# Attention stage of a fused four-layer kernel: a separate order of steps for TensorE, VectorE and ScalarE

## The reference

```python
def _L0_attn_ref(x, Wq, Wk, Wv):
    q = jnp.einsum('bsh,oh->bso', x, Wq)
    k = jnp.einsum('bsh,oh->bso', x, Wk)
    v = jnp.einsum('bsh,oh->bso', x, Wv)
    scores = jnp.einsum('bqh,bkh->bqk', q, k) / jnp.sqrt(jnp.float32(H))
    scores = jnp.where(causal[None, :, :], scores, -jnp.inf)
    att = jax.nn.softmax(scores, axis=-1)
    return jnp.einsum('bqk,bkh->bqh', att, v)

x = x + _L0_attn_ref(_layernorm(x, axis=-1), L0_attn_Wq, L0_attn_Wk, L0_attn_Wv)
```

## Time and profile before

| | before |
|---|---|
| median of 3 executions | 2508.66 us (2501.77 to 2509.47) |
| the profiled execution's own time | 2511.11 us |
| its span | 2509.4 us |
| TensorE matmuls, busy | 2360.6 us (94%) |
| VectorE, busy | 1791.1 us (71%) |
| ScalarE, busy | 1291.6 us (51%) |
| GpSimd, busy | 701.0 us (28%) |
| mean granted TensorE clock | 0.97 |

### The profile page before, as it was taken

One profiled execution on the slowest core, in us unless ns is written; L12 is line 12 of the kernel. 1 busy time (PEld: TensorE's weight loads), 2 busy tenths in 40 slices (PEclk: granted clock), 3 DMA queues, 4 the chain that ended last, 5 costly groups with the idle time before them and its releaser, 6 DMA issues.

```text
span 2509.4 us, 43786 instructions
## 1 busy us (share of the span) xinstructions
PE 2360.6 (94%) x16024; PEld 2182.2 (87%) x16024; DVE 1791.1 (71%) x3323; ACT 1291.6 (51%) x2027; POOL 701.0 (28%) x468
## 2 busy tenths in 40 slices
PE   7999995899999969999999999998999999999999
PEld 6888885899999968988988988987988998899998
DVE  5776775899999866565575574665788787877774
ACT  4445443344444325464464554564666665655554
POOL 1111111444454423023123122122344442321110
PEclk9999997999999989999999999996999999999999
DMA  5000000000000000000000000002000010000001
GB/s 182 0 0 0 0 0 20 1 0 0 0 0 0 1 17 1 13 8 13 13 4 17 13 4 17 8 13 81 26 18 22 20 50 28 1 26 26 25 25 34
DMA packets 43259, 45.69 MB, mean 18 GB/s; under 512 B 3120, under 2 KB 41904, under 8 KB 43184
## 3 DMA queue, kind: packets, MB, share of 16 engines
q1 hardware_dynamic: 43184, 44.69, 5.5%
HBM read 27.90 MB, written 16.78 MB: 18 GB/s over the span
## 4 chain that ended last, share of the span: by engine, by line
PE 51%; DVE 5%; issue 3%; ACT 2%; POOL 1%; DVEq 0%; ACTq 0%; POOLq 0%
PE m_ps_z L1859 12%; PE p_ps_a L1641 4%; PE p_ps_feat L279 4%; PE p_ps_a L1698 4%; PE p_ps_feat L281 3%; PE p_ps_feat L280 3%; PE m_ps_wide L279 3%; PE m_ps_wide L281 3%; PE m_ps_wide L280 3%; PE p_ps_a L1579 2%; PE p_ps_turn L1685 2%; PE m_ps_wide L1837 1%; PE m_ps_wide L1838 1%; PE m_ps_n L1820 1%; PE p_ps_b L279 1%
## 5 line engine op out<-in xcount | busy, mean ns | idle before, releaser
L1951 DVE TENSOR_TENSOR m_a_lo<-m_a,m_a_hi 128x512 fp32r<-128x512 f32 x256 | 201.2, 803 | 144.0 <-ACT m_a_hi L1911 140.1
L1859 PE MATMUL m_ps_z<-m_w_hi,m_a_hi 128*128 128x256 f32 x1024 | 290.7, 284 | 1.5 <-DVE m_a_lo L1951 0.9
L1859 PE MATMUL m_ps_z<-m_w_hi,m_a_lo 128*128 128x256 f32 x1024 | 288.0, 281 | 0.0
L1859 PEld LDWEIGHTS m_ps_z<-m_w_hi,m_a_hi 128*128 128x128 f32 x1024 | 192.3, 188 | 13.5 <-DVE d_w_lo L2468 1.9
L1859 PEld LDWEIGHTS m_ps_z<-m_w_hi,m_a_lo 128*128 128x128 f32 x1024 | 192.7, 188 | 0.0
L1907 ACT ACTIVATE m_a<-m_ps_wide,d_b,d_w_gain 128x512 f32<-128x512 f32 x128 | 99.8, 780 | 135.8 <-PE m_ps_wide L281 131.7
L1324 POOL TENSOR_TENSOR p_kf<-p_kf,p_k_shift 128x1024 f32<-128x1024 f32 x64 | 119.4, 1903 | 155.5 <-DVE p_k_shift L1459 155.5
L1859 PE MATMUL m_ps_z<-d_w_lo,m_a_hi 128*128 128x256 f32 x512 | 144.7, 283 | 0.0
L1859 PE MATMUL m_ps_z<-m_w_lo,m_a_hi 128*128 128x256 f32 x512 | 143.6, 280 | 0.0
L1641 PE MATMUL p_ps_a<-p_ctx_pair,p_kf 128*128 128x34 f32 x1024 | 128.4, 283 | 0.0
L1641 PEld LDWEIGHTS p_ps_a<-p_ctx_pair,p_kf 128*128 128x128 f32 x1024 | 127.7, 203 | 0.4
(11 more groups left out here) (350 smaller groups left out, 8027.4 us busy)
## 6 DMA issues: line engine op xcount, KB each, us to landing
residual<-in_x SPq DMA_DIRECT2D x8, 1024.0 KB, 11.8
attn<-p_attn SPq DMA_DIRECT2D x32, 256.0 KB, 2.2
m_attn<-attn SPq DMA_DIRECT2D x16, 512.0 KB, 3.8
out<-residual SPq DMA_DIRECT2D x16, 512.0 KB, 2.9
raw_weights<-in_d_q SPq DMA_DIRECT2D x2, 1024.0 KB, 7.2
m_attn<-in_d_scale SPq DMA_DIRECT2D x3, 512.0 KB, 4.0
raw_weights<-in_m_w1T SPq DMA_DIRECT2D x1, 1024.0 KB, 5.0
raw_weights<-in_m_w2T SPq DMA_DIRECT2D x1, 1024.0 KB, 7.9
```

Of the source, the lines that this page charges most:

```text
L1859: mm = pe.matmul(z, a, w[:, f, :], start=(f == 0 and k == 0 and j % 2 == 0), stop=(f == FC - 1 and k == 2), skip_group_check=True)
L1951: dve.tensor_tensor(self.a2[1][:, f, :], self.a[f % RING][:, :], self.a2[0][:, f, :].bitcast(F32), ALU.subtract).then_inc(self.a_lo, 1)
```

## The change

VectorE gets an order of its own, and the steps that `schedule` used to append are now in the tables, so that each engine can place them freely. TensorE's order stays the same step by step.

```diff
-        ORDER = "s2 s3 t0 t1 n0 s4 w0 w1 n1 t2 t3 s5 w2 w3 n2 t4 s6 w4 t5 n3 n4 s7 t6 w5 n5 n6"
-
-        ORDER_OF_SCALAR = "s2 s3 t0 t1 t2 s4 t3 s5 t4 s6 t5 n3 n4 s7 t6 n5 n6"
+        ORDER_OF_TENSOR = "s2 s3 t0 t1 s4 w0 w1 t2 t3 s5 w2 w3 t4 s6 w4 t5 s7 t6 w5 T0 T1 w6 t7 P0 P1 w7 T2 T3"
+        ORDER_OF_VECTOR = "s2 s3 t0 t1 N0 s4 t2 w0 t3 w1 s5 N1 w2 w3 N2 t4 s6 w4 t5 s7 t6 w5 T0 T1 w6 t7 P0 P1 w7 T2 T3"
+        ORDER_OF_SCALAR = "s2 s3 t0 t1 t2 s4 t3 s5 t4 s6 t5 N3 N4 t6 s7 T0 T1 N5 N6 t7 P0 P1 T2 T3"
         STEPS = {"s": "scores", "t": "turn", "w": "weigh"}
...
-        def schedule(tile, front, skip_turn, order=ORDER):
+        def schedule(tile, front, skip_turn, order):
...
-                    else:
-                        ahead(e)
-                ahead("t0", "t1")
-                tile(b, "weigh", TB - 2)
-                tile(b, "turn", TB - 1)
-                ahead("p0", "p1")
-                tile(b, "weigh", TB - 1)
-                ahead("t2", "t3")
+                    elif not last:
+                        front(b + 1, e[0].lower(), int(e[1:]))
```

More of the change, by code:

```diff
@@ L434, in body @@
             def body(b, last):
[L435 to L438, removed]
                 def beside(m):
@@ L619, in _ @@
             dve.sem_inc(fp4_weights.quantised, 1)
-            schedule(tile, front, lambda eng: skip_uses(eng, turned_lo))(dve)
+            schedule(tile, front, lambda eng: skip_uses(eng, turned_lo), ORDER_OF_VECTOR)(dve)
         @block.scalar
@@ L746, in front @@
                     mm.then_inc(proj_done, 1)
-            schedule(tile, front, lambda eng: skip_uses(eng, turned))(pe)
+            schedule(tile, front, lambda eng: skip_uses(eng, turned), ORDER_OF_TENSOR)(pe)
         core.ctx = outer
```

## The result

| | before | after |
|---|---|---|
| median | 2508.10 us (2501.77 to 2509.47, 6 executions) | 2491.18 us (2486.83 to 2495.17, 6 executions) |
| span of the profiled execution | 2509.4 us | 2492.0 us |
| mean granted TensorE clock | 0.970 | 0.971 |
| one batch of attention in the loop | 46.88 us | 44.96 us |

The ratio after to before is 0.9936, with a 95% interval of 0.9924 to 0.9948: 13 to 19 us less. The forecast was 2494.3 us, that is 14.4 us less, in a range of 2487 to 2502. A second set with the changed kernel gave 2488.68 against 2504.09 us, ratio 0.9935 (0.9917 to 0.9954).

What follows compares the result with a forecast made beforehand. TensorE was taken to bound attention, so only closing its gaps could pay: 7 x (0.83 + 1.01) = 12.9 us plus 1.47 in the last batch, together 14.4 us, giving 2494.3 us in a range of 2487 to 2502.

Steps and rivals of the forecast that it cites:

- Gap 1: TensorE's wait before w2, 1.48 us a batch; t2's low part ahead of w0 on VectorE closes it.
- t3's copy: On VectorE, t3 ahead of w1: an added wait of 0.3 us, w1's addition just meeting w3; counted as nothing.
- The chain to t4 and the wait before w4: VectorE's unbroken work from t3's to t4's low part makes TensorE wait a new 0.65 us before w4.
- Gap 2: TensorE's wait before T0, 1.01 us a batch; ScalarE copying t6 ahead of s7's exponential closes it.
- VectorE's part: VectorE's new order in seven batches: 0.83 us each is left of 1.48 after the new wait before w4.
- The last batch: In attention's last batch only the wait before w6 closes, 1.47 us; w7's wait stays.
- Cost nothing: ScalarE's copies T0 and T1 ahead of n5 and n6 cost nothing; s7's delayed exponential is covered.
- the first (no wait before w4, 2489.8): Rival: no new wait before w4 in attention, gain 18.9 us, 2489.8 us; chance 7%.
- The second: Rival: VectorE's part gives everything back before w4, only ScalarE's pays; gain 8.5 us, 2500.1 us; chance 13%.
- The third: Rival: VectorE's instructions don't overlap, chain to w4 1.28 us longer; gain 5.4 us, 2503.3 us; chance 3%.
- the fifth: Rival: TensorE's clock falls in attention once a batch, costing 27.2 us; kernel slower at 2521.5 us; chance 5%.
- The fourth: Rival: later layers give part back through clock falls; 7.6 us left, about 2501.1 us; chance 12%.

Runs made afterwards that it cites:

- ScalarE's part alone: ScalarE's new order with VectorE in the old one, against the kernel before: batch 45.72 us, whole 2494.84 us, ratio 0.9955.
- VectorE's part alone: VectorE's new order with ScalarE in the old one, against the kernel before: batch 46.12 us, whole 2502.07 us, ratio 0.9983.

## Why the prediction was right

The mechanism came as it was forecast: two waits gone, a smaller one before w4, and a batch of 44.96 us where 45.0 were named. Two terms were mis-sized, by 0.15 us too little in ScalarE's part and 0.07 too much in VectorE's; they go against each other and are named below. That the whole time came within 3 us of the forecast is in part luck, as it wanders by 8. Point by point, by the prediction's own steps:

- **Gap 1, t2 ahead of w0.** Forecast 1.48 us closed; w2 follows s5 after 0.06. t2's low part starts right behind s4's maximum and lasts 0.55, as priced.
- **t3's copy.** Forecast an added wait of 0.3 on VectorE and w1's addition "just meeting" w3. The wait is 0.26; w1's addition ends at 178.37, and w3 starts at 178.53 instead of 178.40. Moving w1 ahead of t3 takes this wait away, so the addition is its cause. Three small things were off. The estimate of 1.3 us for w2's nine matmuls was too long: from 177.28 to the 178.40 that was due it is 1.12. The 0.71 taken for w1 runs to the next start, and the addition ends 0.08 behind that. And w3 starts 0.15 behind the end of the addition, which wasn't counted. So w1 is just late, not just in time. The prediction said that such a wait would be taken out of w4's; the two together are 0.69 where 0.65 was forecast. Moving w1 alone ahead of t3 shortened the batch by 44.96 - 44.61 = 0.35, what it takes off the chain.
- **The chain to t4 and the wait before w4.** Forecast 6.63 us from t3's low part to the end of t4's (182.9 to 189.53); measured 183.58 - 176.97 = 6.61. Forecast wait 0.65, measured 0.56, with w3's 0.13 ahead of it. The kernel with t4 ahead of n2 shows that the chain is the cause and not ScalarE's copy.
- **Gap 2, t6 ahead of s7.** Forecast 1.01, measured 1.16 by ScalarE's part alone. This term was mis-sized. The wait before T0 was 1.01, but T0 and T1 behind it took 200.61 - 199.68 = 0.93 us to the next matmul, and now take 192.75 - 191.96 = 0.79. Of these 0.14, 0.05 is the first transpose after the wait, with 0.16 to the next start instead of 0.11. The other 0.09 is at T1. The prediction said that the first bank is what T0 needs and left out that T1 behind it needs the second, which VectorE freed only at 199.54 + 0.55 = 200.09. VectorE and then TensorE of the kernel before, in narrow windows (a row of merged neighbours begins with the oldest one still running, so the two rows of TensorE begin with T0's last and T1's first transpose), and TensorE of the changed kernel at the same two:

```profile
199.54 0.55 DVE L573 TENSOR_TENSOR a_probsT_lo<-a_ps_turn,a_probsT_hi 128x384 fp32r<-128x384 f32 x1
...
200.06 0.80 PE L719 MATMUL a_ps_turn<-ident,a_xn 128*128 128x128 f32 x5
...
200.23 0.63 PE L719 MATMUL a_ps_turn<-ident,a_xn 128*128 128x128 f32 x4
```

```profile
192.28 0.60 PE L708 MATMUL a_ps_turn<-ident,a_xn 128*128 128x128 f32 x4
...
192.39 0.49 PE L708 MATMUL a_ps_turn<-ident,a_xn 128*128 128x128 f32 x3
```

From T0's last to T1's first it is 0.17 before and 0.11 now, and T1's second is 0.03 late as well. The view of waits lists none for T1. It rests on the place and on T1 starting 0.15 behind that low part in every batch of the loop, while in the changed kernel, where the low part is long done, the delay is absent.
- **VectorE's part.** Forecast 0.83, measured 0.76. Its waits came to what was forecast: w2's 1.49 gone, 0.12 and 0.54 new before w3 and w4 in the kernel with VectorE's part alone. The missing 0.07 is that two steps, w3 and w4, now start from a wait instead of w2 alone. Behind a wait the second matmul follows 0.05 to 0.08 later than it would.
- **The last batch.** Forecast 1.47, and no new wait; measured 1.5 to 1.7 (next point). Its wait before w6 is gone, w7's stays at 1.57, as here in TensorE's list of the changed kernel:

```profile
376.13 0.38 PE L279 MATMUL a_ps_out<-a_v_hi,a_probsT_hi 128*128 128x256 f32 x1 [1.57 <-DVE a_probsT_lo L562]
```

- **The sum.** Forecast 14.4 in attention; measured 369.65 - 354.55 = 15.1. 7 x 1.92 = 13.4, which leaves 1.7 for the last batch; with ScalarE's part alone 9.66 - 7 x 1.16 leaves 1.5. The whole fell by 16.9 in the first set and 15.4 in the second.
- **Cost nothing:** T0 and T1 ahead of n5 and n6, confirmed by its own experiment. The exponential of s7, delayed by the copies, cost nothing either: neither t7 nor P0 waits.

Of the rivals, the first (no wait before w4, 2489.8) is nearer in whole time than the forecast to the median of the first set, and is wrong all the same: the trace has that wait. In the second set it is the other way round: 18.9 and 14.4 us less than 2504.09 would be 2485.2 and 2489.7, and 2488.68 was measured. A whole time alone, with 8 us of wander, couldn't have told them apart. The second and third (VectorE's part worth nothing or less) are refuted by that part's own 0.76 us a batch. The third was the strict form of what the Trainium skill says in "VectorE: DVE Perf Modes", section "The DRAIN you can't avoid". That section itself adds that an instruction that isn't held starts earlier, and the trace agrees with this: the chain took 6.61 us where its durations and inner waits one behind the other would have taken about 7.8, so here neighbours do overlap. The clock in attention stayed at 1.00, which refutes the fifth. The fourth, as priced, left 7.6 us of the gain; the whole fell by 13 to 19 us, with 15.1 in attention, so it didn't come. A smaller effect of the later layers, of either sign, stays undecided, since they differ by 8 us between two executions of the kernel before.

## What to carry to other kernels

Where several engines follow one table of steps, ask of each wait of the busiest engine which piece of the waited-for engine's list stood ahead without being needed, and price the whole list from there to the next piece that is waited for: the work moved out of the way has to go somewhere, and here 0.7 of 1.5 us came back two steps later. Start-to-start times of neighbours in the trace priced such a chain to 0.02 us, where durations and waits added up would have been 19% too long (7.8 for 6.61 us). Where two steps one behind the other each need a bank, look at both waits: the one that the view names first can hide a second. And read a change of a microsecond in a loop from the loop's period, not from the whole time.

## What the hardware showed beyond the forecast

TensorE restarted from a wait is slow at first by a little: the first transpose of T0 was followed after 0.16 us behind its wait and after 0.11 in a stream; the first matmul of w2 after 0.22 us behind a wait and 0.17 in the last batch, where it didn't wait. With w3's first matmul, 0.19 for 0.12, a gap costs 0.05 to 0.08 us more than its length.

Not every wait is handed over at the same speed. w2 and w4 start 0.05 us behind the end of the low part that they wait for, and so does T0. w3 starts 0.15 us behind the end of w1's addition (178.37 to 178.53), in the kernel with n1 right behind s4 w2 starts 0.15 behind w0's (182.14 to 182.29), and T1 0.15 behind the second low part. Both values repeat in every batch of the loop. What sets the one or the other, no run here isolates.

The same kernel's later layers took 2105.1 and 2097.0 us in two profiled executions, with attention equal to 0.01 us and mean clocks of 0.970 and 0.973. At 2509 us, 0.003 of clock is 7.5 us, about the size of the wander. Twelve executions of the kernel with VectorE's part alone go the same way: spans of 2501.2 to 2502.9 us at clocks of 0.971 and 0.972, and of 2494.3 to 2497.0 at 0.974 and 0.975. What moves the clock from one execution to the next, no run here shows.
